# First layer of a four-stage model: loop over head pairs written out batch by batch, with the norms, gates and weight turning set between its steps

## The chip, the cores and the metric

The program runs on one core of a Trainium2 chip. Its engines work side by side and wait for each other by semaphores: TensorE (PE in the rows; PEld is its loading of weights), VectorE (DVE), ScalarE (ACT), GpSimd (POOL), and SyncE (SP), which here only issues transfers. PE's results go to PSUM, of which the kernel uses eight banks of 128 x 512 floats (`ps`); all other tiles named here are in SBUF. The metric is the device time of one execution in microseconds. Lower is better.

## The reference

The input `x` has 2 batches of 1024 tokens with 128 values, all in float32. Four stages follow each other, each as `x = x + layernorm(stage(layernorm(x)))`.

```python
def _L0_attn_ref(x, Wq, Wk, Wv):          # H, R = 8, 64; d = 128
    Q = (x @ Wq.T).reshape(b, n, H, R)
    K = (x @ Wk.T).reshape(b, n, H, R)
    V = (x @ Wv.T).reshape(b, n, H, d)
    attn = softmax(einsum('bnhr,bmhr->bhnm', Q, K), axis=-1)
    return einsum('bhnm,bmhd->bnd', attn, V)     # heads are summed

def _L0_ffn_ref(x, gate_w, w1, b1, w2, b2, w3, b3, sw1, sw2, sw3):   # E = 8 experts, top 2
    scores = softmax(xt @ gate_w.T)
    weights, idx = top_k(scores, 2)
    xs = xt[:, None, :] * weights[:, :, None]
    for e in range(E):
        y += sum((silu(xs @ w1[e].T + b1[e]) @ w2[e].T + b2[e]) * (xs @ w3[e].T + b3[e]) * (idx == e))
    z = silu(xt @ sw1.T) * (xt @ sw2.T) @ sw3.T
    return y + z
```

The third stage is a causal attention with 16 heads and a bias by distance. The fourth is two layers of windowed attention with a gated feed-forward. The change leaves these two as they are.

## The kernel before, in words

All of it is one function, `build`, with one instruction stream per engine, written by hand. The order in the code is the order on the engine, and nothing reorders it. What is late on one engine delays all that stands behind it there.

**First attention.** Two heads are a pair, and one pair of one batch is a block: 8 blocks. A loop over the 4 pairs (`Fori(0, PAIRS)`) holds two blocks, batch 0 and batch 1, so that q, k, v of one block are projected while the other still runs. GpSimd copies the pair's weights to fixed places (`a_weights`, `wq_st`, `wk_st`, `wv_st`). A block has 8 slots. In slot i PE makes the scores of 128 queries for both heads (`scores(i)`, L671, banks 0 to 3), turns two rows of probabilities made before (`turn`, L682, banks 4 and 5), and weights values with turned ones (`weigh`, L640). DVE takes the row maxima (L1269), ScalarE the exponentials with their sums (L1726), DVE divides (L1276), and both copy the turned halves back (`copy_out`). Each of PE's float32 products runs as two passes, and the rows count passes.

A block's output is 1024 queries in four quarters, c = 0 to 3, with two heads each: `weigh(m, b, c, head, k0, k1)` adds key tiles k0 to k1. Quarters 0 and 1 lie in the two halves of bank 6, quarters 2 and 3 in those of bank 7, and `add_out` (L1256) adds a full bank to `yT` on DVE. Quarter 2's second head and quarter 3 come only in the tail and in slots 0 to 2 of the next block. In block 0 the same code runs with nothing to weight: it works on cleared buffers. In the tail PE projects the next block's q (L609), k (L615) and v (L627); the last block projects a ninth one, which nobody uses.

```python
for i in range(QT):
    if i == 1:
        turn(0)
    scores(i)
    if i == 0:
        weigh(m - 1, 1 - b, 2, 1, 3, 8)
        weigh(m - 1, 1 - b, 3, 0, 0, 3)
    ...
    else:
        turn(2 * i - 2)
        weigh(m, b, (i - 3) // 2, (i - 3) % 2, 0, 6)
        turn(2 * i - 1)
        weigh(m, b, (i - 3) // 2, (i - 3) % 2, 6, 8)
```

**Ahead of it.** Both batches of `x` are loaded and normalised (`norm_in(0)`: DVE statistics L1171, ScalarE's root, DVE L1187, PE's transposes). PE turns the attention weights (L590) and all 31 blocks of expert and gate weights (L604, L601), and DVE copies these back.

**Behind it** come, one after the other, for all 16 tiles: `norm_out(0)` and the residual sum on GpSimd, `norm_in(1)`, the gate product (L733) and the choice of two experts on DVE, meanwhile the shared expert (`shared_up`, `shared_down`, L744 to L753), and the gate weights turned (L853). Then the experts: 32 units of one expert and 512 tokens, 16 for batch 0 and 16 for batch 1. In each PE spreads the gate's weights (L765, L766) and makes three products (L782, L788, L772), DVE has `scale`, a product with the mask, and `product`, ScalarE a copy and a Silu, and GpSimd sums into `yT` (`gather`, L2042). Norms of batch 0 behind the experts are already set between the units of batch 1 (`half_stats`, `half_aggr`, `half_norm`, `half_xn`), with the root as a power of -0.5 on GpSimd (`half_rstd`, L2050).

Of the kernel before, what the change touches and what calls it, by code (L numbers as in the profile page):

```python
# [13 lines left out]
P = 128  # L14
# [5 lines left out]
CH = 512  # L20
# [108 lines left out]
def build(nc, a, out):  # L129
    with ExitStack() as ctx:  # L130
# [16 lines left out]
        eps_c = sb("eps_c", [P, 1])  # L147
        ps = ctx.enter_context(nc.psum_tensor("ps", [P, 8, CH], F32))
# [12 lines left out]
        wq_st = sb("wq_st", [P, P])  # L161
        wk_st = sb("wk_st", [P, P])
        wv_st = sb("wv_st", [P, 256])

        w0qk = sb("w0qk", [P, 2, PAIRS + 1, P])
        w0q, w0k = w0qk[:, 0, :, :], w0qk[:, 1, :, :]
        w0v = sb("w0v", [P, PAIRS + 1, 256])
# [36 lines left out]
        gw = probs[:, 0, :].rearrange("p (n t e) -> p n t e", t=TILES, e=E0)  # L204
# [89 lines left out]
        s_ld_x = sem("s_ld_x")  # L294
# [18 lines left out]
        s_y = [sem(f"s_y{n}") for n in range(4)]  # L313
# [3 lines left out]
        s_a_wst = sem("s_a_wst")  # L317
# [17 lines left out]
        s_a_pz = sem("s_a_pz")  # L335
        s_a_oadd = sem("s_a_oadd")
        s_a_ozero = sem("s_a_ozero")
# [117 lines left out]
        def _(sp):  # L455
            for b in range(BATCH):
                sp.dma_start(x_sb[:, b * QT:(b + 1) * QT, :],
                             a["L0_attn_x"][b].rearrange("(t p) d -> p t d", p=P)).then_inc(s_ld_x, 16)
# [3 lines left out]
            sp.dma_start(wnat[:, 8:16, :], a["L0_attn_Wv"].rearrange("(n p) d -> p n d", p=P)).then_inc(s_ld_w0, 16)  # L462
# [67 lines left out]
            sp.wait_ge(s_y[2], 1)  # L530
# [23 lines left out]
        NU = 16  # L554
# [14 lines left out]
        def _(pe):  # L569
# [17 lines left out]
            pe.wait_ge(s_ld_w0, 16 * 4)  # L587
            for g in range(4):
# [3 lines left out]
            norm_in(0)  # L592

            pe.wait_ge(s_ld_f, 16 * 12)
            for g in range(9):
                if g < 4:
                    pe.wait_ge(s_w0t, 1)
                else:
                    pe.wait_ge(s_ft, g - 3)
                if g == 8:  # L600
                    ins = pe.transpose(ps[:, 4, 0:STRIP], gnat[:, :], ident[0:STRIP, 0:STRIP])  # L601
                else:
                    for i in range(min(4, 30 - 4 * g)):
# [9 lines left out]
            def a_proj_k(b):  # L613
# [1667 lines left out]
```

## Time and profile before

| | |
|---|---|
| median of 3 runs (lowest, highest) | 1608.4 us (1608.1, 1611.72) |
| the profiled execution, own time | 1610.09 us |
| its span, first to last instruction | 1608.0 us |
| instructions | 25414 |
| PE busy | 1383.7 us, 86% |
| DVE busy | 1049.2 us, 65% |
| ACT busy | 779.7 us, 48% |
| POOL busy | 387.2 us, 24% |
| mean granted clock of PE | 0.929 |
| PE's share of the chain that ended last | 62% |

Shares are means over stages with different limits, so the table says little on its own. The first attention, the gap behind it and the experts are read apart below. A granted clock of 1.00 is 2.4 GHz, of 0.50 is 1.2 GHz; a value between is a mean over a stretch that had both.

### The profile page before, as it was taken

To read this page: it belongs to the slowest core of one execution; us is meant where nothing else is said; L and a number is where in the kernel's file an instruction comes from. 1 tells how busy PE (TensorE), PEld (TensorE's weight loads), DVE (VectorE), ACT (ScalarE), POOL (GpSimd) and SP (SyncE) were. 2 spreads that over 40 slices of the span, in tenths; PEclk is the share of its full clock that TensorE was granted. 3 is DMA by queue.
4 is the path that set the end of the run, shared out by engine and by line. 5 is a ranking of instruction groups with operands and counts; after the bars stand their busy time and mean duration, and the time that the engine had idled before them with its cause. 6 is when DMAs were issued, how large, how long until landed. Compare 5 with 4: busy or idle time off the path is not lost.

```text
span 1608.0 us, 25414 instructions
## 1 busy us (share of the span) xinstructions
PE 1383.7 (86%) x9075; PEld 818.4 (51%) x9075; DVE 1049.2 (65%) x2238; ACT 779.7 (48%) x1658; POOL 387.2 (24%) x268
## 2 busy tenths in 40 slices
PE   6999999999999958997799999983688868788866
PEld 4777777777676733332233333322356643466542
DVE  6767767767676663666666676706688744788644
ACT  2444445444454413342245666663477743488731
POOL 2000000000000011345400000001588810688801
PEclk9999999999999978998678999997799979799978
DMA  5000000000000000002023111002000000000000
GB/s 132 1 1 1 0 0 0 0 0 0 0 0 0 0 0 0 1 1 92 12 74 86 40 46 44 5 2 60 1 1 0 1 1 1 1 0 0 1 0 26
DMA packets 23650, 25.44 MB, mean 16 GB/s; under 512 B 5570, under 2 KB 20108, under 8 KB 22284
## 3 DMA queue, kind: packets, MB, share of 16 engines
q1 hardware_dynamic: 23580, 24.51, 5.2%
q8 instruction: 44, 0.72, 0.2%
q14 instruction: 26, 0.21, 0.0%
HBM read 20.11 MB, written 4.39 MB: 15 GB/s over the span
## 4 chain that ended last, share of the span: by engine, by line
PE 62%; POOL 15%; DVE 10%; issue 7%; ACT 4%; DMA 2%; POOLq 0%; SPq 0%; DVEq 0%; ACTq 0%
PE ps L640 14%; PE ps L671 8%; PE ps L682 8%; POOL d_rn L2152 5%; PE ps L952 4%; POOL probsT L2163 4%; PE ps L911 4%; PE ps L932 3%; PE ps L788 2%; POOL q_st L2150 2%; POOL k_st L2150 2%; PE ps L782 2%; PE ps L627 2%; PE ps L772 2%; PE ps L1153 1%
## 5 line engine op out<-in xcount | busy, mean ns | idle before, releaser
L1881 ACT ACTIVATE probsT<-ps 128x512 f32<-128x512 f32 (+1 forms) x304 | 163.7, 576 | 111.0 <-PE ps L936 98.4
L1269 DVE TENSOR_REDUCE negmax<-ps 128x1 f32<-128x1024 f32 x128 | 150.8, 1220 | 76.1 <-PE ps L671 76.1
L1726 ACT ACTIVATE probs<-ps,negmax 128x1024 f32<-128x1024 f32 x128 | 142.8, 1115 | 75.8 <-DVE negmax L1269 75.5
L1732 ACT COPY probsT<-ps 128x512 f32<-128x512 f32 x128 | 75.0, 586 | 177.7 <-PE ps L682 177.7
L682 PEld LDWEIGHTS ps<-ident,probs 128*128 128x128 f32 x1024 | 114.7, 141 | 58.4 <-issue 53.5
L911 PE MATMUL ps<-arena 76*128 76x512 bf16 (+3 forms) x384 | 116.1, 363 | 26.8 <-DVE cmax L1477 20.4
L682 PE MATMUL ps<-ident,probs 128*128 128x128 f32 x1024 | 136.3, 276 | 0.0
L640 PE MATMUL ps<-probsT,v_nat 128*128 128x256 f32 x554 | 129.9, 380 | 0.0
L671 PE MATMUL ps<-k_st,q_st 64*128 64x512 f32 x512 | 127.2, 615 | 2.2 <-DVE v_st L1248 1.4
L1477 DVE CUSTOM_DVE_ANT_0 k_st<-ps,rel 128x256 f32<-128x256 f32 (+7 forms) x128 | 96.8, 756 | 47.9 <-PE ps L911 46.4
L1477 DVE CUSTOM_DVE_ANT_0 q_st<-ps,rel 128x256 f32<-128x256 f32 (+7 forms) x128 | 96.7, 756 | 45.2 <-PE ps L911 44.2
L932 PE MATMUL ps<-arena 79*128 79x512 bf16 (+3 forms) x384 | 115.1, 343 | 7.7 <-ACT probsT L1881 5.4
L640 PE MATMUL ps<-probsT,v_st 128*128 128x256 f32 x512 | 120.8, 380 | 0.0
L1954 ACT ACTIVATE probsT<-ps,d_nm,d_rn 128x128 f32<-128x128 f32 x256 | 113.4, 466 | 11.5 <-DVE d_nm L1611 11.5
L1282 DVE COPY probsT<-ps 128x512 f32<-128x512 f32 x128 | 87.9, 687 | 45.6 <-PE ps L682 44.6
L1996 POOL COPY wq_st<-w0qk 128x128 f32 (+1 forms) x5 | 1.5, 293 | 476.2 <-PE ps L671 463.6
L640 PEld LDWEIGHTS ps<-probsT,v_nat 128*128 128x128 f32 x554 | 100.9, 190 | 14.4 <-issue 3.0
L640 PEld LDWEIGHTS ps<-probsT,v_st 128*128 128x128 f32 x512 | 92.9, 190 | 13.3 <-issue 3.0
L1276 DVE TENSOR_SCALAR probs<-probs,rrow 128x1024 f32<-128x1024 f32 x128 | 96.4, 753 | 4.5
L1031 PE MATMUL ps<-arena 128*128 128x512 f32 x128 | 71.7, 689 | 30.0 <-ACT arena L1969 15.5
L2152 POOL TENSOR_TENSOR d_rn<-ss,half_c 128x16 f32<-128x16 f32 x32 | 93.1, 2910 | 0.4
L911 PEld LDWEIGHTS ps<-arena 76*128 76x128 bf16 x384 | 31.9, 102 | 101.7 <-DVE cmax L1477 71.2
(259 smaller groups left out, 2665.7 us busy)
## 6 DMA issues: line engine op xcount, KB each, us to landing
arena<-c_parts SPq DMA_DIRECT2D x32, 192.0 KB
arena<-c_parts SPq DMA_DIRECT2D x16, 128.0 KB
arena<-in_L_ffn_w_dram SPq DMA_DIRECT2D x3, 512.0 KB
c_parts<-probsT SPq DMA_DIRECT2D x2, 768.0 KB, 3.5
arena<-in_c_far_dram SPq DMA_DIRECT2D x16, 96.0 KB
c_parts<-work SPq DMA_DIRECT2D x2, 768.0 KB, 11.2
work<-in_L_ffn_wqkv_dram SPq DMA_DIRECT2D x1, 1536.0 KB
x_sb<-in_L_attn_x_dram SPq DMA_DIRECT2D x2, 512.0 KB, 4.8
```

Of the source, the lines that this page charges most:

```text
L640: ins = pe.matmul(ps[:, 6 + c // 2, (c % 2) * HC:(c % 2 + 1) * HC], a_v[b][:, kt, head * P:(head + 1) * P], a_pT[:, c % 2, head, kt, :], s ...
L671: ins = pe.matmul(ps[:, 2 * head + n, :], q_st[r:r + R0, i * P:(i + 1) * P], k_st[r:r + R0, n * CH:(n + 1) * CH], start=True, stop=True)
L682: ins = pe.transpose(ps[:, 4 + half, i * P:(i + 1) * P], probs[:, u % NPB, kt * P:(kt + 1) * P], ident[:, :])
L911: ins = pe.matmul(ps[:, 2 * (u % 2) + i, 0:e - i * CH], c_q2[buf][0:SHALLOW, j, qt * P:(qt + 1) * P], c_k2[buf][0:SHALLOW, j, i * CH:e], s ...
L932: ins = pe.matmul(ps[:, 4 + c % 2, i * n:(i + 1) * n], c_k2[buf][0:DEEP, j0 + i, kt * P:(kt + 1) * P], c_q2[buf][0:DEEP, j0 + i, q0:q0 + n ...
L1269: dve.tensor_reduce(negmax[:, u:u + 1], s2, AX_X, ALU.max, negate=True)\
L1276: dve.tensor_scalar(probs[:, u % NPB, :], probs[:, u % NPB, :], rrow[:, u:u + 1], None, ALU.mult).then_inc(s_a_norm, 1)
L1477: dve.tensor_tensor_reduce(c_dump[u % 2][:, 0:w], s2, rel[:, SEQ - w:SEQ], 1.0, -3.0e38, ALU.add, ALU.max, cmax[:, s % 2, m:m + 1]).then_i ...
L1726: act.activation(probs[:, u % NPB, :], s2, ACT.Exp, bias=negmax[:, u:u + 1], accum_out=rowsum[:, u:u + 1]).then_inc(s_a_exp, 1)
L1881: act.activation(c_p[:, kt % 2, j0:j0 + heads, q0 - kt * P:q0 - kt * P + n], ps[:, 4 + c % 2, 0:heads * n].rearrange("p (h n) -> p h n", n ...
L1954: ins = act.activation(d_p[:, par, h, :], ps[:, 6 + h // 4, (h % 4) * P:(h % 4 + 1) * P], ACT.Exp, bias=d_nm8[:, par, h:h + 1], scale=d_rn ...
L2152: pool.tensor_tensor(d_rn[:, par, :], ss[:, par, :], half_c[:, :], ALU.pow).then_inc(s_d_rn, 1)
```

## The change

The loop becomes plain code, `for m in range(BLOCKS)`, that runs all four pairs of batch 0 and then those of batch 1. Projections read the turned weights where they lie, and GpSimd's copies go. Block 0 skips the weighting of nothing, and the last block projects nothing.

At eight slots times eight blocks there are 64 numbered slots, and each of three engines has a function `a_piece(m, i)` that does at some of them a piece of other work: the nine groups of expert weights (PE in slots 0 to 6, 11 and 12, copied back by ScalarE in place of DVE), the input norm of batch 1 (14 to 22), the output norm of batch 0's attention (35 to 38), its next input norm (40 to 46), and its gates (51 to 63). Batch 1's output norm lies within the shared expert's products, and its next input norm and gates between the first 16 expert units. All pieces use bank 7. For that the quarters lie differently: 0, 1 and 2 one after another in the first half of bank 6, and only quarter 3 in bank 7, each read out by DVE on its own (256 columns), so that PE may start a quarter in bank 6 only when DVE has read the one before.

Batch 0 of `x` is asked for first and batch 1 behind the attention weights. ScalarE loads its tables by dummy operations at the start, and copies the turned wq and wk.

```diff
-            with pe.Fori(0, PAIRS) as p:
-                for b in range(BATCH):
...
+            for m in range(BLOCKS):
+                for i in range(QT):
+                    if i == 1:
+                        turn(m, 0)
+                    scores(m, i)
+                    if i == 0:
+                        weigh(m - 1, 2, 1, 6, 8)
+                        weigh(m - 1, 3, 0, 0, 6)
...
+                    a_piece(m, i)
+                if m + 1 < BLOCKS:
...
+                    a_proj_v(m + 1)
+                    weigh(m, 2, 1, 0, 6)
...
+                if k0 == 0:
...
+                    if c < 3 and head == 0 and 4 * m + c >= 1:
+                        pe.wait_ge(s_a_oadd, 4 * m + c if c else 4 * m - 1)
...
-                    ins = pe.matmul(ps[:, 6 + c // 2, (c % 2) * HC:(c % 2 + 1) * HC],
-                                    a_v[b][:, kt, head * P:(head + 1) * P],
+                    ins = pe.matmul(ps[:, 6 + c // 3, 0:HC],
+                                    a_v[m % 2][:, kt, head * P:(head + 1) * P],
...
+            def a_piece(m, i):
+
+                slot = QT * m + i
+                if slot < 7:
+                    turn_f(slot)
...
+                if slot == 51:
+                    gate(0, 0)
+                    gate(0, 4)
+                if slot == 62:
+                    turn_g(0, 0, 7)
...
-            a_weights(0)
```

**At the end of a block** PE's rows before are these, block 0 into block 1 (L627 projects v, L640 weights, L671 are scores, L682 turned probabilities, REGISTER_ALU the loop's counters):

```order
L627 MATMUL ps<-wv_st,xT 128x256 x8
L635 REGISTER_ALU
L640 MATMUL ps<-probsT,v_st 128x256 x3
L671 MATMUL ps<-k_st,q_st 128x512 x4
L640 MATMUL ps<-probsT,v_st 128x256 x5
L635 REGISTER_ALU
L640 MATMUL ps<-probsT,v_st 128x256 x3
L679 REGISTER_ALU
L682 MATMUL ps<-ident,probs 128x128 x8
```

and with the change (L669 projects v, L698 weights, L718 scores, L733 turned probabilities):

```order
L669 MATMUL ps<-w0v,xT 128x256 x8
L698 MATMUL ps<-probsT,v_st 128x256 x6
L718 MATMUL ps<-k_st,q_st 128x512 x4
L698 MATMUL ps<-probsT,v_st 128x256 x8
L733 MATMUL ps<-ident,probs 128x128 x8
L718 MATMUL ps<-k_st,q_st 128x512 x4
L733 MATMUL ps<-ident,probs 128x128 x8
L698 MATMUL ps<-probsT,v_st 128x256 x5
```

The tail weights six key tiles in place of three. Slot 0 keeps eight. Slot 1 weights five in place of seven (its rows before, x5 and x2, follow the ones shown), and slot 2 five in place of six.

**At the end of attention** PE's rows before run from the last projection of v to the first shared product (L583 and L575 turn the two norms, L733 is the gate product, L744 the shared expert):

```order
L627 MATMUL ps<-wv_st,xT 128x256 x8
L635 REGISTER_ALU
L640 MATMUL ps<-probsT,v_nat 128x256 x3
L654 REGISTER_ALU
L654 COMPARE_AND_BRANCH
L640 MATMUL ps<-probsT,v_nat 128x256 x21
L583 MATMUL ps<-ident,yT 128x128 x16
L575 MATMUL ps<-ident,xn 128x128 x16
L733 MATMUL ps<-gateT,xT 128x8 x16
L744 MATMUL ps<-xT,arena 128x512
```

and with the change (L733 and L698 as above, L756 turns gate weights, L861, L862 and L870 are the shared expert):

```order
L698 MATMUL ps<-probsT,v_nat 128x256 x2
L756 MATMUL ps<-ident,work 32x128 x4
L733 MATMUL ps<-ident,probs 128x128 x8
L698 MATMUL ps<-probsT,v_nat 128x256 x8
L733 MATMUL ps<-ident,probs 128x128 x8
L698 MATMUL ps<-probsT,v_nat 128x256 x16
L861 MATMUL ps<-xT,arena 128x512
L862 MATMUL ps<-xT,arena 128x512
L861 MATMUL ps<-xT,arena 128x512
L862 MATMUL ps<-xT,arena 128x512
L870 MATMUL ps<-probsT,arena 128x512
L619 MATMUL ps<-ident,yT 128x128 x8
```

The projection is gone, the two norms and the gate product stand earlier or later, and the shared expert follows the last weighting.

**DVE in a late slot of the last block**: before, any slot ended so (L1274 and L1276 divide, L1282 copies a turned half, L1269 are row maxima):

```order
L1274 RECIPROCAL rrow<-rowsum 128x1
L1276 TENSOR_SCALAR probs<-probs,rrow 128x1024
L1280 ISA
L1282 COPY probsT<-ps 128x4x128
L1274 RECIPROCAL rrow<-rowsum 128x1
L1276 TENSOR_SCALAR probs<-probs,rrow 128x1024
L1267 REGISTER_ALU
L1269 TENSOR_REDUCE negmax<-ps 128x1
```

and with the change slot 62 ends so (L1406 and L1408 divide, L1414 copies, L1396 adds a quarter, L1454 and L1455 write the last part of the gate weights, L1401 row maxima):

```order
L1406 RECIPROCAL rrow<-rowsum 128x1
L1408 TENSOR_SCALAR probs<-probs,rrow 128x1024
L1414 COPY probsT<-ps 128x4x128
L1406 RECIPROCAL rrow<-rowsum 128x1
L1408 TENSOR_SCALAR probs<-probs,rrow 128x1024
L1396 TENSOR_TENSOR yT<-ps,yT 128x256
L1454 CAST work<-work 128x64
L1455 CAST work<-work 128x8x8
L1401 TENSOR_REDUCE negmax<-ps 128x1 x2
```

Behind the second division stand a quarter's sum and two casts, for which PE's L756 of slot 62 waits.

## Rows read from the trace of the kernel before

**Rows 1.** Busy us (instructions) by stretch: PE, PEld, DVE, ACT, POOL; clock, DMA share, GB/s.

```profile
0.00:35.00 35.00, 19.41 (x87) 14.67 (x88) 22.27 (x73) 7.43 (x10) 9.10 (x14) 0.95 0.61 152
100.47:493.14 392.67, 391.99 (x2064) 282.54 (x2065) 277.61 (x408) 179.24 (x300) 2.61 (x9) 1.00 0.00 0
567.40:620.40 53.00, 28.84 (x109) 16.72 (x108) 30.77 (x171) 11.77 (x20) 7.00 (x6) 0.71 0.00 0
620.40:688.40 68.00, 67.57 (x160) 24.47 (x161) 40.27 (x69) 21.79 (x37) 22.22 (x18) 0.95 0.00 1
```

**Rows 2.** Timeline of PE, scores in block 0: start us, duration us, instruction.

```profile
35.03 1.99 PE L671 MATMUL ps<-k_st,q_st 64*128 64x512 f32 x8 [1.41 <-DVE v_st L1248]
41.62 1.99 PE L671 MATMUL ps<-k_st,q_st 64*128 64x512 f32 x8
47.59 1.99 PE L671 MATMUL ps<-k_st,q_st 64*128 64x512 f32 x8
54.00 1.99 PE L671 MATMUL ps<-k_st,q_st 64*128 64x512 f32 x8
...
83.09 1.99 PE L671 MATMUL ps<-k_st,q_st 64*128 64x512 f32 x8
100.47 1.09 PE L671 MATMUL ps<-k_st,q_st 64*128 64x512 f32 x3
```

**Rows 3.** Timeline, all engines, slot 6 of block 0.

```profile
77.73 1.09 PE L682 MATMUL ps<-ident,probs 128*128 128x128 f32 x8
77.83 2.36 DVE L1269 TENSOR_REDUCE negmax<-ps 128x1 f32<-128x1024 f32 x2 [1.23 <-PE ps L671]
78.66 2.76 PE L640 MATMUL ps<-probsT,v_st 128*128 128x256 f32 x12
...
80.30 1.11 ACT L1726 ACTIVATE probs<-ps,negmax 128x1024 f32<-128x1024 f32 x1
...
83.12 0.75 DVE L1276 TENSOR_SCALAR probs<-probs,rrow 128x1024 f32<-128x1024 f32 x1
```

**Rows 4.** Timeline, tail of block 0.

```profile
90.27 1.88 PE L609 MATMUL ps<-xT,wq_st 128*128 128x512 f32 x4
...
95.45 3.62 PE L627 MATMUL ps<-wv_st,xT 128*128 128x256 f32 x16
...
99.11 1.22 DVE L1248 COPY v_nat<-ps 128x1024 f32<-128x1024 f32 x1 [1.91 <-PE ps L627]
```

**Rows 5.** Timeline of DVE, first norm, and the second norm's scaling.

```profile
6.73 3.19 DVE L1171 BATCH_NORM_STATS2 stats<-x_sb 128x6 f32<-128x128 f32 x16 [5.84 <-DMA x_sb<-in_L_attn_x_dram]
9.96 1.17 DVE L1174 BATCH_NORM_AGGREGATE mv<-stats 128x2 f32<-128x6 f32 x16
...
584.36 4.20 DVE L1187 TENSOR_SCALAR xn<-x_sb,mv,rstd 128x128 f32<-128x128 f32 x16
```

**Rows 6.** Timeline, end of attention to the shared expert.

```profile
557.01 10.52 PE L640 MATMUL ps<-probsT,v_nat 128*128 128x256 f32 x48
...
590.40 4.45 PE L733 MATMUL ps<-gateT,xT 128*128 128x8 f32 x32 [0.67 <-ACT xT L1693]
...
603.78 1.28 ACT L1761 ACT_TABLE_LOAD   x1 [7.93 <-DVEq L1345]
```

**Rows 7.** Timelines, expert units 18 to 20 with a norm between them.

```profile
694.95 1.02 PE L782 MATMUL ps<-probsT,arena 128*128 128x512 f32 x2
...
697.83 1.66 POOL L2050 TENSOR_TENSOR rstd<-rstd,half_c 128x8 f32<-128x8 f32 x1
698.26 1.02 PE L782 MATMUL ps<-probsT,arena 128*128 128x512 f32 x2
...
699.46 1.26 POOL L2042 TENSOR_TENSOR yT<-yT,probsT 128x512 f32<-128x512 f32 x1
699.52 3.07 DVE L1443 TENSOR_SCALAR xn<-x_sb,mv,rstd 128x128 f32<-128x128 f32 x8 [0.21 <-POOL rstd L2050]
...
703.25 1.13 PE L782 MATMUL ps<-probsT,arena 128*128 128x512 f32 x2
```

More of the change, by code:

```diff
@@ new lines, in gate @@
+            def gate(b, t0):
+                if t0 == 0:
+                    pe.wait_ge(s_xT, group_no(1, b, 1))
+                    if b == 0:
+                        pe.wait_ge(s_a_oadd, 24)
+                for t in range(t0, t0 + 4):
+                    ins = pe.matmul(ps[:, 7, t * E0:(t + 1) * E0], xT[:, (QT * b + t) * P:(QT * b + t + 1) * P],
+                                    gateT[:, :], start=True, stop=True)
+                if t0 == 4:
+                    ins.then_inc(s_logits, 1)
@@ L1203, in norm_out, with half_stats, half_aggr, out_stats @@
                         ins.then_inc(s_yn, 1)
+            def half_stats(kind, k, b, g, src):
+                for i in range(4):
+                    ch.link(dve.bn_stats(stats[:, QT * b + 4 * g + i, :], src(i)))
+            def half_aggr(b, g=None):
+                part = tiles_of(b, g)
+                ch.settle()
+                for t in range(part.start, part.stop):
+                    ins = dve.bn_aggr(mv[:, t, :], stats[:, t, :])
+                ins.then_inc(s_hvar, 1)
+            def out_stats(k, b, g, bank):
+                dve.wait_ge(s_yp, group_no(k, b, g))
+                half_stats("out", k, b, g, lambda i: ps[:, bank, i * P:(i + 1) * P])
@@ new lines, in gate_scores, with gate_best @@
+            def gate_scores(b):
+                half = tiles_of(b)
+                dve.wait_ge(s_gexp, b + 1)
+                ch.step(dve.tensor_reduce(gsum[:, half], gw[:, 1], AX_X, ALU.add))
+                ch.step(dve.reciprocal(gmax[:, half], gsum[:, half]))
+                ch.step(dve.tensor_tensor(gw[:, 2], gw[:, 1], per_token(gmax[:, half]), ALU.mult))
+            def gate_best(b):
+                for t in range(QT):
+                    ch.link(dve.max(gw[:, 3, t, :], gw[:, 2, t, :]))
+                ch.settle()
@@ L1345, in _ @@
-            dve.sem_inc(s_G, 1)
+            in_stats(0, 0, 0)
+            in_stats(0, 0, 1)
+            ch.settle()
+            for t in range(QT):
+                ins = dve.bn_aggr(mv[:, t, :], stats[:, t, :])
+            ins.then_inc(s_var, 1)
+            dve.wait_ge(s_sd, 1)
+            ch.step(dve.reciprocal(rstd[:, 0:QT], sd[:, 0:QT]))
+            half_xn(0, 0, 0, 0)
+            half_xn(0, 0, 1, 0)
+            turned_w0(0)
+            turned_w0(1)
+            a_evac_k(0)
+            a_evac_v(0)
@@ L1347, in shared @@
+            add_out(BLOCKS - 1, 2)
+            add_out(BLOCKS - 1, 3)
             def shared(k):
@@ L1426, in _ @@
+            units(0, UB, piece)
             shared(4)
```

1002 lines of the change are left out of this document (576 added, 426 removed).

## The prediction

> **What bounds the kernel now.** I read the stages first, in the table of busy time by stretch [rows 1]. Blocks 1 to 6 of the first attention keep TensorE (PE) at work 391.99 of 392.67 us at a granted clock of 1.00, its level of 2.4 GHz. Whoever shortens that part must take PE work out. On either side lie 35.0 us before the first scores, and 53.0 us between the last weighting (567.4) and the first expert unit (620.4), in which PE is busy for 28.8 us at a clock of 0.71. Those two gaps need only better order.
>
> Second, the starts of the scores in block 0: eight slots and a tail [rows 2]. Slots 0, 1 and 2 take 6.59, 5.97 and 6.41 us; the four from 54.00 to 83.09 take 7.27 each; slot 7 with the tail takes 17.38. The next block begins 65.44 us after this one, and the six blocks of [rows 1] take 392.67, again 65.44 each. A pass of the loop holds two blocks, so a branch back costs nothing that can be seen, and writing the loop out gains nothing by itself.
>
> Third, one steady slot [rows 3], S (75.81) being the start of its scores, 7.28 ahead of the next ones. PE's work in it: scores 4 x 0.43 (two heads side by side), 16 transposes of 0.107, 16 passes of 0.215, together 6.9 of the 7.27. VectorE (DVE) sat idle for 1.23 us before the row maxima, which end at S+4.38. ScalarE's second exponential then needs 1.1, and its sum lands near S+5.7, where PE wants it at S+7.27. So per slot DVE has 1.23 us idle, and may be some 1.3 us late beyond that before PE waits. The chain's 5.7 us is also the shortest slot.
>
> **The start.** DVE begins its statistics at 6.73, when both halves of x are in; 16 tiles take 3.19 [rows 5]. With one batch asked for first I take x at 4.9 (it then shares the queues with less), and go by halves of the rows: statistics 1.6, aggregation 0.6, root and reciprocal 0.7, eight normalisations 2.1, so 9.9. The last four transposes and their copy end at 11.5, and the eight transposes of Wv, which the code puts ahead of the projections, at 12.6. Then come the projections, 1.9 + 1.9 + 3.6 [rows 4], hence first scores at 20.5 in place of 35.03: **-14.5**. The 30 turned expert weights and DVE's clearings leave this path. Bounds: all projections at half clock, 7 later (-7.5); x sooner, -16.
>
> **Attention.**
> - The eighth block no longer projects a ninth: 1.72 + 1.72 + 3.44 = **-6.9** [rows 4].
> - Block 0 weighted nothing useful 21 times (42 passes, 9 us of PE). But slot 0 waits for its first normalised row anyway, and slots 1 and 2 cannot go under 5.7. That leaves 0.25 + 0.7, **-0.9**.
> - Six passes move into the tail, four leave slot 1, two leave slot 2 (the order above). The tail was all but covered: the second half of v is copied by 100.33, scores start at 100.47 [rows 4, 2]. So the tail grows by 6 x 0.215 less 0.15 = 1.1. Slot 1 gives back 0.25 (then the chain holds it), slot 2 0.43. Net 0.45 at each of 7 boundaries, **+3.2**.
> - Pieces on PE. Nine groups of turned weights, of which the six in slots 3 to 6, 11 and 12 count, 2.4 in all; those in slots 0 to 2 lie in PE's new gaps. Eight groups of four transposes for norms and gates at 0.45, 3.6. The gate product of one batch, half of 4.45, so 2.2 [rows 6]. Sum 8.2; nothing can cover them in slots where PE is the bound.
> - Pieces on DVE. Four statistics take 0.8 and four normalisations 1.05 [rows 5]; from PSUM I estimate 1.3, for a gate step 0.5 to 0.7, and for a quarter of the output 0.4 in every second slot. All of DVE's work in the seam was 30.8 for both batches [rows 1], so one batch's norms and gates are at most 15, spread over 30 slots. They lie in the 1.23 of idle time and the 1.3 of play. Slots 16, 40 and 41 are themselves short, and I give them 1.3. Slot 62 is the exception: PE turns the gate weights at the end of its slot, but DVE writes the last part of them only behind its own last multiply, which ends at S'+0.8 (S' = start of the next scores [rows 3]), a quarter and two casts. That is 1.7 of wait on PE. With PE's 8.2: **+11.2**.
> - Slots 0 to 2 of block 0 now leave PE idle half of the time. Where it idled in the seam, its clock was 0.71 [rows 1]. I charge **+3.0** for one or two spells at 1.2 GHz (0 to 8).
>
> **The seam.** Of the 53.0 us, batch 1's output norm and four shared products stay behind the last weighting. Counted from it: first product 0.9, table load 1.28 [rows 6], Silu 0.6, DVE's product 0.7; PE goes on with batch 1's transposes, three more pairs of products and down products. The third of these waits for ScalarE's copy of y, at +11. DVE: statistics until +7.5, aggregation until +8.1; POOL's root, 1.66 [rows 7] and a short sum ahead of it, until +10.3; eight normalisations until +12.9, the last product, the first scaling at +14.3. First unit at +14.6, so 14.6 - 53.0 = **-38.4**. If the root is not waited for, it is -40; if all of it runs at half clock, -32.
>
> **First 16 expert units.** A unit takes 3.31 where nothing is put in [rows 7]. The second half of the experts already carries such a norm: the unit with eight normalisations and eight transposes took 4.99, which prices the same piece in the first half at +1.7. The gate product adds 2.2 and turning the gate weights 0.9. Around the one Exp stand two table loads of 1.28; ScalarE has room for half of them before Silu is late, +1.3. Other steps 0.4: **+6.5**.
>
> In that unit eight normalisations took 3.07 where they take 2.10 alone (half of 4.20), and a sum on POOL of 1.26 us ran at their start [rows 7, 5]. The Trainium skill (SBUF — State Buffer, Who interferes with whom) states that DVE in a two-port mode and GpSimd hold one pair of ports in turn, each for a whole instruction; by that rule, the row agrees. By it the four residual sums that POOL now makes during attention could each hold up DVE's multiply for a whole sum, and the total would be up to 5 us worse if nothing covered it. By the slot's rows its play covers one such hold-up, and I leave the sum as it is.
>
> **The sum.** -14.5 - 6.9 - 0.9 + 3.2 + 11.2 + 3.0 - 38.4 + 6.5 = -36.8. Behind the 16th unit nothing moves but wait counts and banks' names. The profiled execution took 1610.1 us (span 1608.0), so it becomes 1573.3; it lay 1.7 above the median, so I forecast a median of **1572**. Less than 0.3% (5 us) from 1608.4 cannot be told from no change.
>
> **Rivals.**
> 1. *As summed*, 1565 to 1581: 0.62.
> 2. *DVE's play is too small, or PE's clock falls.* Slots 35 to 38 carry 1.3 us each against 0.85 or 1.23 of idle time, and POOL's hold-ups come on top; or PE, thinner in places, is granted half clock for longer. For it: DVE is busy 277.6 of 392.7 us as it is [rows 1]. Against: each overrun is small and an empty slot wins back 1.2. Price: 0.25 us in each of 64 slots (16), or three spells of 10 us at half the speed (15): 1582 to 1592, 0.18.
> 3. *More is hidden.* The pieces on PE fill the 0.4 of gaps per slot, the clock stays up, x lands early. Then 11.2, 3.0 and 6.5 shrink by half: 1553 to 1564, 0.14.
> 4. *Slower: quarters share a bank.* Quarters 0, 1 and 2 of every block now build up in one half bank, and PE may not start one before DVE has read the last. By the slot, DVE is through at S'+1.2 and PE starts at S'+2.85: 1.6 us of margin at 24 hand-overs. This decides only where each read comes 3.4 us later than I reckon (1.75 beyond the margin, 24 x 1.75 = 42 us against 37 gained): 1614 or more, 0.04. For it stands that DVE works in strict order, so that a late piece delays the read as well.
> 5. *Nothing moves*: the seam's work comes back inside attention at full price. Against it, 24 of the 53 us were PE's idle time: 1608, 0.02.
>
> Chances: faster 0.94, same 0.02, slower 0.04. The range, 1559 to 1587, takes in the start at half clock (+7) and half of case 2, and the pieces at nothing (-13).
>
> **What would show it.** Right: first scores at 20 to 21 us; later blocks of 65.9 plus their pieces, with empty slots 3 to 6 still at 7.27 and tails longer by 1.1; PE waiting for DVE some 1.7 us in slot 62; the last weighting's end near 560, the first expert unit near 575, the 17th near 648, and all behind as before but 40 us earlier. Wrong: slots of 7.5 or more with DVE as releaser, PE waits on the reads of quarters, half clock inside attention, or a seam over 20 us.

## The result, and the profile after

The changed kernel takes 1568.12 us in the median of 4 runs (1564.41 to 1569.39), the kernel before 1608.25 in as many on the same chip: a ratio of 0.9744, 95% interval 0.9721 to 0.9768. Forecast were 1572 and a range of 1559 to 1587. Measured once more beside later kernels it took 1568.45 (0.9736, 0.9714 to 0.9758).

Its profiled execution took 1564.41 us, span 1562.6. Busy time by stretch, with the columns of [rows 1]:

```profile
0.00:19.40 19.40, 12.04 (x48) 8.73 (x48) 7.23 (x30) 7.64 (x11) 0.30 (x5) 1.00 0.99 244
19.40:88.65 69.25, 62.69 (x338) 44.48 (x337) 46.86 (x69) 33.67 (x57) 0.99 (x3) 0.98 0.04 9
88.65:491.82 403.17, 397.96 (x2110) 287.60 (x2109) 292.30 (x500) 181.78 (x308) 9.48 (x12) 1.00 0.00 1
561.60:576.30 14.70, 12.67 (x35) 5.31 (x34) 8.45 (x30) 4.74 (x7) 5.31 (x5) 0.96 0.00 0
576.30:650.60 74.30, 70.41 (x194) 26.91 (x192) 53.99 (x134) 27.19 (x45) 25.16 (x22) 0.99 0.00 1
```

Start and seam are short, and the stretches between are longer. To see where, take the start of each slot's scores (L718 on PE) and of each expert unit (L901) and subtract. The starts of the eight blocks and the 17th unit, in both kernels, worked out so from the timelines:

```
            first  block 1  2       3       4       5       6       7       weighting ends  unit 1  unit 17
before      35.03  100.47   165.92  231.37  296.81  362.25  427.69  493.14  567.54          620.44  688.49
after       19.41  88.65    155.44  222.90  289.19  356.34  423.86  491.82  561.61          576.31  650.60
```

The start, in the timelines of DVE and PE ([rows 5, 4] are the counterparts):

```profile
5.23 1.64 DVE L1329 BATCH_NORM_STATS2 stats<-x_sb 128x6 f32<-128x128 f32 x8 [4.33 <-DMA x_sb<-in_L_attn_x_dram]
...
8.15 2.14 DVE L1364 TENSOR_SCALAR xn<-x_sb,mv,rstd 128x128 f32<-128x128 f32 x8
...
12.42 1.88 PE L648 MATMUL ps<-xT,w0qk 128*128 128x512 f32 x4
...
19.41 1.99 PE L718 MATMUL ps<-k_st,q_st 64*128 64x512 f32 x8
```

Before, PE's timeline had the turned expert weights ahead of the projections, which began at 25.41, and a wait within them:

```profile
20.46 4.79 PE L604 MATMUL ps<-ident,arena 128*128 128x128 f32 x30 [2.42 <-DVE w0v L1218]
...
31.62 1.99 PE L627 MATMUL ps<-wv_st,xT 128*128 128x256 f32 x8 [0.79 <-DVE k_st L1244]
```

So 13.0 of the 15.6 us lie ahead of the projections and 2.6 behind their start.

In attention an empty slot 3 to 6 takes 7.27 as before. The boundary of two blocks and the first slots of the next, in the timeline of PE (blocks 0 and 1; [rows 2, 4] are their counterparts):

```profile
77.33 1.88 PE L648 MATMUL ps<-xT,w0qk 128*128 128x512 f32 x4
...
82.51 3.62 PE L669 MATMUL ps<-w0v,xT 128*128 128x256 f32 x16
85.96 2.75 PE L698 MATMUL ps<-probsT,v_st 128*128 128x256 f32 x12
88.65 1.99 PE L718 MATMUL ps<-k_st,q_st 64*128 64x512 f32 x8
...
95.19 1.99 PE L718 MATMUL ps<-k_st,q_st 64*128 64x512 f32 x8
...
100.86 1.99 PE L718 MATMUL ps<-k_st,q_st 64*128 64x512 f32 x8 [0.50 <-ACT probs L1944]
102.78 1.09 PE L733 MATMUL ps<-ident,probs 128*128 128x128 f32 x8
103.70 1.46 PE L698 MATMUL ps<-probsT,v_st 128*128 128x256 f32 x6
105.00 0.60 PE L733 MATMUL ps<-ident,probs 128*128 128x128 f32 x4
105.89 0.66 PE L733 MATMUL ps<-ident,probs 128*128 128x128 f32 x4 [0.28 <-DVE probsT L1414]
106.38 1.03 PE L698 MATMUL ps<-probsT,v_st 128*128 128x256 f32 x4
107.34 1.99 PE L718 MATMUL ps<-k_st,q_st 64*128 64x512 f32 x8
```

Twelve passes now stand in the tail, where six stood. Slot 1 (from 95.19) takes 5.67, slot 2 (from 100.86) 6.48: it has two passes fewer than before, yet is no shorter than the old 6.41. The old slot 2 (from 113.03), in PE's timeline before:

```profile
115.87 2.32 PE L640 MATMUL ps<-probsT,v_st 128*128 128x256 f32 x10
118.03 1.04 PE L682 MATMUL ps<-ident,probs 128*128 128x128 f32 x8
118.91 0.60 PE L640 MATMUL ps<-probsT,v_st 128*128 128x256 f32 x2
```

The second half of the slot's last turning needs VectorE's copy, and that copy stands behind both row maxima. Before, ten passes stood ahead of this turning and PE came to it late enough not to wait; two stood behind. Now six stand ahead, PE waits 0.28 there (105.89), and four stand behind. So of the 0.86 us of the four passes taken out ahead, about half is lost at the wait, and the two passes added behind it cost 0.43: nothing is left.

Slot 62, the last weighting and the seam, same view, with [rows 6] as counterpart; the turning of the gate weights is L756, the unit's first product L901:

```profile
538.65 1.03 PE L698 MATMUL ps<-probsT,v_nat 128*128 128x256 f32 x4
541.17 0.61 PE L756 MATMUL ps<-ident,work 128*32 128x128 f32 x4 [1.50 <-DVEq L1459]
541.71 1.99 PE L718 MATMUL ps<-k_st,q_st 64*128 64x512 f32 x8
...
554.53 7.07 PE L698 MATMUL ps<-probsT,v_nat 128*128 128x256 f32 x32
561.44 1.02 PE L861 MATMUL ps<-xT,arena 128*128 128x512 f32 x2
...
571.46 1.10 PE L870 MATMUL ps<-probsT,arena 128*128 128x512 f32 x2 [0.40 <-ACT yT L2004]
...
574.73 1.80 PE L870 MATMUL ps<-probsT,arena 128*128 128x512 f32 x2 [1.63 <-DVE probsT L1552]
576.31 1.91 PE L901 MATMUL ps<-probsT,arena 128*128 128x512 f32 x2
```

### The profile page after: what moved, and what is told of

Its sections match the earlier page's. It is cut to its first block, busy times and chain, and to the rows that moved or that the text cites. A ratio compares the mean times of both kernels' runs of the same rounds, so it can differ in the third digit from the quotient of the medians.

```text
span 1562.6 us, 24586 instructions
## 1 busy us (share of the span) xinstructions
PE 1352.1 (87%) x9009; PEld 799.1 (51%) x9009; DVE 1042.3 (67%) x2249; ACT 782.3 (50%) x1668; POOL 386.9 (25%) x264
## 4 chain that ended last, share of the span: by engine, by line
PE 58%; POOL 16%; DVE 11%; issue 8%; ACT 5%; DMA 1%; POOLq 0%; SPq 0%; DVEq 0%; ACTq 0%
PE ps L698 12%; PE ps L718 8%; PE ps L733 6%; POOL d_rn L2383 5%; PE ps L1070 4%; POOL probsT L2394 4%; PE ps L1029 4%; PE ps L1050 3%; POOL q_st L2381 2%; DVE negmax L1401 2%; POOL k_st L2381 2%; PE ps L907 2%; PE ps L901 2%; PE ps L669 2%; PE ps L1273 2%
## 5 line engine op out<-in xcount | busy, mean ns | idle before, releaser
L1401 DVE TENSOR_REDUCE negmax<-ps 128x1 f32<-128x1024 f32 x128 | 150.7, 1219 | 72.3 <-PE ps L718 72.1
L733 PEld LDWEIGHTS ps<-ident,probs 128*128 128x128 f32 x1024 | 114.7, 141 | 66.0 <-issue 43.8
L733 PE MATMUL ps<-ident,probs 128*128 128x128 f32 x1024 | 138.6, 277 | 6.6 <-DVE probsT L1414 3.3
L718 PE MATMUL ps<-k_st,q_st 64*128 64x512 f32 x512 | 128.5, 620 | 5.9 <-ACT probs L1944 5.9
L698 PE MATMUL ps<-probsT,v_st 128*128 128x256 f32 x512 | 120.8, 380 | 0.0
L698 PE MATMUL ps<-probsT,v_nat 128*128 128x256 f32 x512 | 120.2, 380 | 0.0
L2195 ACT ACTIVATE probsT<-ps,d_nm,d_rn 128x128 f32<-128x128 f32 x256 | 113.4, 467 | 11.6 <-DVE d_nm L1803 11.6
L1414 DVE COPY probsT<-ps 128x512 f32<-128x512 f32 x128 | 87.7, 685 | 43.4 <-PE ps L733 43.3
L698 PEld LDWEIGHTS ps<-probsT,v_st 128*128 128x128 f32 x512 | 92.9, 190 | 13.3 <-issue 3.0
L698 PEld LDWEIGHTS ps<-probsT,v_nat 128*128 128x128 f32 x512 | 93.1, 190 | 12.7 <-issue 2.3
L1408 DVE TENSOR_SCALAR probs<-probs,rrow 128x1024 f32<-128x1024 f32 x128 | 96.4, 753 | 4.5
## 6 DMA issues: line engine op xcount, KB each, us to landing
c_parts<-work SPq DMA_DIRECT2D x2, 768.0 KB, 11.2
```

Source lines behind the costliest of these rows:

```text
L698: ins = pe.matmul(ps[:, 6 + c // 3, 0:HC], a_v[m % 2][:, kt, head * P:(head + 1) * P], a_pT[:, c % 2, head, kt, :], start=(head == 0 and k ...
L718: ins = pe.matmul(ps[:, 2 * head + n, :], q_st[r:r + R0, i * P:(i + 1) * P], k_st[r:r + R0, n * CH:(n + 1) * CH], start=True, stop=True)
L733: ins = pe.transpose(ps[:, 4 + half, i * P:(i + 1) * P], probs[:, u % NPB, kt * P:(kt + 1) * P], ident[:, :])
L1401: dve.tensor_reduce(negmax[:, u:u + 1], s2, AX_X, ALU.max, negate=True).then_inc(s_a_negmax, 1)
L1408: dve.tensor_scalar(probs[:, u % NPB, :], probs[:, u % NPB, :], rrow[:, u:u + 1], None, ALU.mult).then_inc(s_a_norm, 1)
L2195: ins = act.activation(d_p[:, par, h, :], ps[:, 6 + h // 4, (h % 4) * P:(h % 4 + 1) * P], ACT.Exp, bias=d_nm8[:, par, h:h + 1], scale=d_rn ...
```

## The experiments

All started from one of the two kernels. The times are medians (of one run each in 6 and 8); the ratios are to the kernel before on the same chip, 0.9744 (0.9721 to 0.9768) for the changed kernel, and as the chips differ they compare kernels better than the times. The slots and units are worked out from the timelines of the profiled executions, as above.

**1. The loops written out, nothing else** (kernel before).

```diff
-            with pe.Fori(0, PAIRS) as p:
+            for p in range(PAIRS):
```
(and the same for the other three engines)

> The kernel before, with the four loops over pairs of blocks written out and nothing else changed: same instructions in the same order, waits on constants in place of registers. Theory (the prediction's reading that the branch back costs nothing): every block still takes 65.44 us and the time stays at 1608.3, within 2 us. Rival A (the branch did cost something on some engine's path): blocks 1 to 6 fall under 65.3 and the time by 1 us or more. Rival B (straight code has to be fetched all the time and that costs): blocks grow past 65.6, the time by 1 us or more, with idle time of PE that no semaphore ends.

Measured: 1607.99 against 1609.98, ratio 0.9993 (0.9971 to 1.0014). Blocks 1 to 6 take 65.37 in place of 65.44; the 0.08 comes off slot 0 of blocks 1 to 7, also where no branch lies ahead, so it is not the branch. The blocks stay between the bounds of Rivals A and B; the whole time cannot tell them apart.

**2. Without useless passes and ninth projection** (kernel before, written out). The passes left out had also cleared part of the bank that the first addition reads, so part of the output is off in this kernel.

```diff
+                if m < 0:
+                    if c == 3 and k1 == QT and head == 1:
+                        pe.sem_inc(s_a_pv, 1)
+                    return
...
-                    a_proj_q(nb)
+                    if not last:
+                        a_proj_q(nb)
```

> The kernel before, written out, and without the 42 passes of block 0 that weight nothing useful and without the ninth projection and its four evacuations. Theory (terms of the prediction): 6.9 less at the end of block 7 and 0.9 less in block 0, so 7.8 us faster, 1600.5, last weighting's end at 559.7 in place of 567.5. Rival A: only the ninth projection counts (-6.9, block 0 unchanged), because slots 0 to 2 of block 0 wait for the first normalised rows or fall to half clock when PE idles there. Rival B: the ninth projection covered ScalarE's and VectorE's last steps, so that only part of 6.9 comes back (-4 or less).

Measured: 1600.87, ratio 0.9947 (0.9927 to 0.9967), 7.1 below the one before. From the start of block 7 to the last weighting's end it is 68.00 in place of 74.32, -6.3. But slots 0 to 2 of block 0 take 6.91, 6.99 and 5.67, 0.6 more than the 18.97 before: a spell at half clock, 3.4 us long from 41.5, fell on the scores of slot 1. Rival A holds for block 0. Part of what block 7 lacks to 6.9 is a wait of 0.33 for ScalarE's copy at its last turning (PE, 550.11), now that no projection lies ahead of it. In the profiled execution the seam also grew by 3.2 (27.3 us at half clock on end behind 567.2, where it was 17.1 and 6.8); the medians do not show that.

**3. Both halves of x first** (changed kernel).

```diff
             load_x(0)
+            load_x(1)
             sp.dma_start(ident[:, :], a["c_ident"]).then_inc(s_ld_w0, 16)
```
(and the later `load_x(1)` taken out)

> The changed kernel, with both batches of x asked for first, as before the change, and the weights of q, k and v behind them. It tells how much of the earlier start comes from asking for one batch alone. Theory: VectorE's statistics begin at 5.23 in the changed kernel and began at 6.73 before; with both halves ahead they begin between 5.3 and 6.7 and the weights land later too, so first scores move from 19.4 to 20.5 to 21.5: 1 to 2 us slower. Rival A: the first half lands as soon as before, since the order in the queue alone decides it, and only the weights come later; the first scores are held by the weights or not at all, 0 to 0.5 us. The rest of the 15.6 us (the turned expert weights and the clearings off the path, half as many tiles) stays in both.

Measured: 1568.59, ratio 0.9753 (0.9734 to 0.9772), no difference to the changed kernel that the runs could tell. In the profiled execution the first scores start at 20.39 in place of 19.41. VectorE's statistics begin at 5.22, as in the changed kernel (5.23). The weights come later, as the timeline of PE shows, first of the changed kernel, then of this one:

```profile
7.23 1.97 PE L625 MATMUL ps<-ident,probsT 128*128 128x128 f32 x8 [7.23 <-DMA probsT<-in_L_attn_Wk_dram]
```
```profile
9.07 1.97 PE L625 MATMUL ps<-ident,probsT 128*128 128x128 f32 x8 [9.07 <-DMA probsT<-in_L_attn_Wk_dram]
```

So asking for one batch gives some 1.0 of the 15.6 us, and by way of the weights. The 1.0 is one pair of profiles: in the nine profiles with the changed order (the changed kernel, its repeat and the runs from 4 on) the first scores start between 18.96 and 19.85, and this turning between 6.88 and 7.40. The order of the queue, not the amount in it, sets when the first half of x is there: the mechanism is Rival A's, with the theory's size. That VectorE could begin 1.5 earlier than before has another cause: before, it waited for both halves.

**4. The old split of passes at the boundary** (changed kernel).

```diff
-                        weigh(m - 1, 2, 1, 6, 8)
-                        weigh(m - 1, 3, 0, 0, 6)
+                        weigh(m - 1, 2, 1, 3, 8)
+                        weigh(m - 1, 3, 0, 0, 3)
...
-                    weigh(m, 2, 1, 0, 6)
+                    weigh(m, 2, 1, 0, 3)
```
(slots 1 and 2 likewise)

> The changed kernel, with the passes of quarters 2 and 3 at a block's boundary divided as before the change (3 in the tail, 5+3 in slot 0, 5+2 in slot 1, 5 and 1 in slot 2). Theory (from the slots as they now stand in the profile): tail 17.4 in place of 18.5, slot 1 back from 5.67 to 5.96, slot 2 back from 6.48 to 6.41, so 0.84 less at each of 7 boundaries, 5.9 us faster. Rival A (the prediction's own term): 0.45 at each, 3.2 us faster. Rival B: with quarters 0 to 2 in one half bank the old split makes PE wait for VectorE's read of quarter 2, and nothing is won or up to 3 us lost.

Measured: 1560.15, ratio 0.9698 (0.968 to 0.9716), 8.0 below the changed kernel (7.4 by the ratios). Tails 17.39, slot 1 at 5.96, slot 2 at 6.41, and no new wait. The last weighting ends 6.8 earlier. Against the kernel before, this part of the change was a loss of 0.84 at each of seven boundaries, 5.9. Against this run it is 0.91, 6.4 in all, because the 0.84 also holds what slot 0 gains in straight code (run 1). The other 0.5 comes from slots 1 and 2 of blocks 2 and 5, which lie behind pieces (6.80 to 6.41 in block 5).

**5. Batch 0's gates behind attention** (changed kernel): product, shift, exponential, choice, parts and turning leave slots 51 to 63; VectorE does them ahead of `shared(2)`.

> The changed kernel, with batch 0's gates (product, shift, exponential, best two, index, the three parts, turning) taken out of slots 51 to 63 and put behind the last weighting, between the shared products; the norms stay inside attention. It asks what hiding the gates was worth. In attention they cost PE 1.69 in slot 51, 2.11 in slot 62 and 0.44 in slot 63, so 4.2 us come back there. In the seam VectorE's gate work is 6.7 us (sum of its rows in slots 52 to 62), of which 2 us fit into its wait for GpSimd's root; then PE's turning and two copies by ScalarE follow, 1.3. Theory: the seam grows from 14.7 to 21 us (20 to 23), net 2 us slower than the changed kernel. Rival A (the seam has room beside VectorE, so that the gates cost little there): seam under 18, net faster by 1 or more. Rival B (the chain of gate steps is one of waits, not of work): seam of 26 or more, net slower by 7 or more, with half clock in it as before.

Measured: 1574.73, ratio 0.9777 (0.9748 to 0.9807), 6.6 slower than the changed kernel (5.3 by the ratios, whose intervals overlap; in the profiled executions the 17th unit starts 8.2 later). The last weighting ends at 557.42, 4.2 earlier, as expected. The seam takes 26.3, not 21: Rival B, though the net loss of the medians stays just under its 7. The timeline shows that ScalarE has its Exp, which needs the gate product, ahead of the table load and the Silus, and that each later step waits for the one before:

```profile
560.69 1.85 PE L740 MATMUL ps<-gateT,xT 128*128 128x8 f32 x16
...
563.36 1.28 ACT L1984 ACT_TABLE_LOAD   x1
...
566.19 2.04 PE L858 MATMUL ps<-probsT,arena 128*128 128x512 f32 x2 [3.66 <-DVE probsT L1532]
568.03 1.91 PE L619 MATMUL ps<-ident,yT 128*128 128x128 f32 x8
...
578.32 1.53 PE L858 MATMUL ps<-probsT,arena 128*128 128x512 f32 x2 [2.96 <-DVE probsT L1532]
```

The table load begins 5.9 us behind the last weighting (before this edit 0.1). PE waits 3.7 us for the first down product, half clock comes with it (6.8 us of it, from 565.2), and the norm's turning (L619) begins 10.6 us behind the last weighting where it began at 4.1, so that its root and all behind come late. 6.7 us of VectorE's work and 1.9 + 0.9 of PE's (product and turning) make the seam 11.6 longer; how much of the 11.6 is the half clock and how much the chain, this run does not separate.

**6. GpSimd's first three sums left out** (changed kernel).

```diff
+                if k in (0, 1, 2):
+                    pool.sem_inc(s_e_y, 1)
+                    return
                 pool.tensor_tensor(y, y, e_t[:, k % 2, :], ALU.add).then_inc(s_e_y, 1)
```

> The changed kernel, leaving out GpSimd's sums of the first three expert units' results (1.27 us each; the output lacks these units), waits and counts kept. It asks why unit 3 takes 5.96 us where 5.0 was forecast: there VectorE's eight normalisations take 4.03 us, while two of GpSimd's sums run. Theory (the two engines hold each other up in the memory they share): the eight take 2.1 to 2.2, and unit 3 falls to 4.1 to 4.9. Rival (VectorE's late start or its own order makes the unit long): the normalisations stay at 3 to 4 us or the unit stays at 5.7 or more.

Measured: unit 3 (units counted from 0) takes 4.18 for 5.96. First the eight normalisations of the changed kernel with the sums on GpSimd (timelines of both engines; in [rows 7] one sum met eight such, and they took 3.07), then those of this kernel:

```profile
588.14 1.27 POOL L2289 TENSOR_TENSOR yT<-yT,probsT 128x512 f32<-128x512 f32 x1
589.58 1.29 POOL L2289 TENSOR_TENSOR yT<-yT,probsT 128x512 f32<-128x512 f32 x1 [0.17 <-POOL yT L2289]
588.21 4.03 DVE L1364 TENSOR_SCALAR xn<-x_sb,mv,rstd 128x128 f32<-128x128 f32 x8 [0.23 <-POOL rstd L2256]
```
```profile
589.56 2.14 DVE L1364 TENSOR_SCALAR xn<-x_sb,mv,rstd 128x128 f32<-128x128 f32 x8 [0.22 <-POOL rstd L2256]
```

Two of eight last 1.3 us each, a whole sum, where one takes 0.33. The theory is shown: 1.9 us of VectorE's time, and 1.8 of the unit's. The time of this kernel, 1568.59 in its one run, says nothing: units 0 and 1 were 1.6 longer in it (6.8 us at half clock from 575.9).

**7. Quarters read 3.6 us later** (changed kernel).

```diff
                     rowmax(m, u + 1)
+                    if i % 2 == 1:
+                        add_out((4 * m + i // 2 - 2) // 4, (i // 2 - 2) % 4)
```
(and the call at the end of the even slots taken out)

> The changed kernel, with VectorE's read of each quarter of the output moved from the end of an even slot to behind the row maxima of the next one. It puts the prediction's slow rival (quarters share a bank) into effect. In the changed kernel the read ends 1.72 before PE starts the next quarter; moved, it ends 3.6 later, 1.9 beyond the margin. Two hand-overs per block have so little room, quarter 0 to 1 in slot 5 and 1 to 2 in slot 7; from 2 to the next block's 0 there are two slots. Theory: PE waits some 1.9 in slots 5 and 7 of each block, 16 times, of which an empty slot gives nothing back: 25 to 32 us slower than the changed kernel. Rival A (24 hand-overs, as the prediction counted): 40 us or more. Rival B (the work behind catches up, since VectorE and ScalarE have slack in a slot): PE waits, but slots grow by under 1 us, less than 15 us in all.

Measured: 1603.26 (1601.41 to 1611.18), ratio 0.9964 (0.9946 to 0.9983), 35 slower than the changed kernel; in the profiled execution the 17th unit starts 40.1 later. PE's timeline in slot 5 of block 1, and of block 2:

```profile
130.75 2.83 PE L698 MATMUL ps<-probsT,v_nat 128*128 128x256 f32 x12 [1.84 <-DVE yT L1396]
```
```profile
201.75 4.51 PE L698 MATMUL ps<-probsT,v_st 128*128 128x256 f32 x12 [1.84 <-DVE yT L1396]
```

Slot 5 and slot 7 with its tail each grow by 2.08, in all blocks: 16 hand-overs, 33 us. The theory had the mechanism and the count, and its 25 to 32 us were too few: a slot grows by more than its wait, and the work behind catches up nothing. Four of those slots grow by some 1.7 more. In each of these four lies a spell of 3.4 us at half clock (from 201.9, 345.2, 509.1 and 563.7), and twelve passes take 4.51 where they take 2.76.

**8. PE filled in slots 0 to 2 of block 0** (changed kernel).

```diff
+                    if m == 0 and i < 3:
+                        for r in range(8):
+                            pe.matmul(ps[:, 6, 0:HC], a_v[0][:, 4 + r % 4, 0:P], xT[:, 0:HC],
+                                      start=True, stop=True, skip_group_check=True)
```

> The changed kernel, with eight more passes of 256 columns on PE at the end of slots 0, 1 and 2 of block 0, whose result is overwritten unread. It asks what the half clock at 25.5 us costs and whether PE's idle time brings it. Now the three slots take 6.92, 6.94 and 6.05. Theory: PE is idle nearly half of the time there; with the passes in its gaps (0.86 a slot) the spell at half clock goes away or moves, and the slots come down to 6.6, 5.9, 6.0, so 1 to 1.5 us less in all. Rival A: the spell stays, whatever PE does behind the scores, and the passes cost their own time at half clock: 1 to 3 us more. Rival B: spell gone, but the slots stay at about 6.9, because VectorE's and ScalarE's chain holds them.

Measured: 1571.54 in one run, slower and not faster. There is no half clock before 578.8, but the slots take 6.83, 6.83 and 9.51. Each of these products is two passes, so the filling cost 3.62 a slot and not the 0.86 that I wrote: more than the gap holds, and in slot 2 all of it is paid. With PE filled the spell is gone, so PE's idle time brings it; on its price the run says nothing.

**9. Three edits together** (changed kernel): the old split; part 1 of the gate weights in slot 60, part 2 in 61; four such products, 1.89 us, in slots 0 and 1 of block 0.

> The changed kernel with three small edits: the old split of passes at a block's boundary, part 1 of batch 0's gate weights moved from slot 61 to 60 and part 2 from 62 to 61, and four products (eight passes, 1.8 us) on PE at the end of slots 0 and 1 of block 0, overwritten unread. Theory: the split gives 6.8 (as its own run showed at the 17th unit), the parts take VectorE's last one out of PE's path in slot 62 (9.38 to 7.7, -1.67), the passes lie wholly in PE's 3 us of idle time and keep the clock at 1.00, so that slots 0 and 1 take 6.5 and 5.9 (-1.4). 17th unit at 640.7 in place of 650.6, time 1558. Rival A (slot 62): the turning waits for something else than the last part, and stays over 9 us. Rival B (the clock): four products are too few, the spell at half clock stays, and slots 0 and 1 sum to 13.8 as before or more.

Measured: 1556.87 (1556.05 to 1557.33), ratio 0.9663 (0.9642 to 0.9685), 17th unit at 640.07. All three came out. Slot 62 takes 7.71, and the turning follows the weighting without a wait:

```profile
529.82 1.03 PE L698 MATMUL ps<-probsT,v_nat 128*128 128x256 f32 x4
530.68 0.60 PE L756 MATMUL ps<-ident,work 128*32 128x128 f32 x4
531.22 1.99 PE L718 MATMUL ps<-k_st,q_st 64*128 64x512 f32 x8
```

The filling costs nothing, and slots 0 and 1 take 6.54 and 5.66 at a clock of 1.00:

```profile
21.59 1.89 PE L836 MATMUL ps<-xT,v_st 128*128 128x256 f32 x8
24.70 1.09 PE L733 MATMUL ps<-ident,probs 128*128 128x128 f32 x8 [1.22 <-DVE probs L1412]
25.73 1.99 PE L718 MATMUL ps<-k_st,q_st 64*128 64x512 f32 x8
```

In the changed kernel a wait of 2.95 stood there, and the scores behind it fell into the spell from 25.5:

```profile
24.93 1.47 PE L733 MATMUL ps<-ident,probs 128*128 128x128 f32 x8 [2.95 <-DVE probs L1408]
26.33 3.25 PE L718 MATMUL ps<-k_st,q_st 64*128 64x512 f32 x8
```

**10. Normalisations dealt out over two units** (on top of 9).

> The one before, and batch 1's eight normalisations of unit 2 dealt out over two units (four on VectorE behind unit 2, four behind unit 3, turned on PE in units 3 and 4), with the gate's product a unit later. Theory: GpSimd's two queued sums then hold up one normalisation each at most while VectorE has a unit's slack for each half; units 3 and 4 take 4.0 to 4.3 each in place of 5.96 and 3.41, so 1 us less (0.5 to 1.5), and the gate's shift by a unit moves nothing. Rival A: unit 3 stays at 5 or more, since both sums still fall into the first four: nothing gained. Rival B: the later gate steps now pile up in unit 7 or the last two and cost 1 us or more there.

Measured: 1558.13, ratio 0.9667 (0.9645 to 0.969): no gain. Units 3 and 4 take 4.93 and 3.89 in place of 5.95 and 3.40, so 0.5 less. Both sums still fall into the first four normalisations, as Rival A has it (its bound, 5 or more for unit 3, was just missed):

```profile
579.44 3.00 DVE L1367 TENSOR_SCALAR xn<-x_sb,mv,rstd 128x128 f32<-128x128 f32 x4 [0.22 <-POOL rstd L2259]
```

GpSimd begins its queued sums with the end of the same root for which VectorE waits, so the first share meets them however the rest is dealt out. One of the other four meets a third sum (2.05 for four, from 584.27). Units 0 and 1 were 2.0 longer in this execution (6.8 us at half clock from 565.9; in 9 it was 3.4).

**11. The changed kernel again.**

> The changed kernel once more, beside the two above on one chip. It asks how much of its time behind the 17th unit is chance. In its first profile that stretch took 912.0 us, in the profile of the kernel before 919.5, with a spell of 17.1 us at half clock at 869.7 that the changed kernel had not. Theory (the spell belongs to an execution, not to a kernel): 17th unit again at 650.6 within 0.5, stretch behind it between 912 and 919, median 1566 to 1570. Rival (the changed kernel avoids it by its work): stretch again 912.0 within 0.5.

Measured: 17th unit at 650.79, the stretch behind it 915.8. The theory holds: 912.0 belonged to one execution.

## Why the prediction was right, point by point

The median came out 4 us under the forecast, by the mechanism forecast; the profiled execution 8.9 under its 1573.3. Up to the 17th unit the sum was -36.8 and -37.9 was measured (688.49 to 650.60). That is closer than its terms: they miss by -1.1 (start), -1.2 (block 0 and clock), +2.7 (split), -1.4 (pieces), +0.2 (seam) and -0.3 (units), which cancel by chance. The signs "near 560", "near 575" and "near 648" don't follow from the sum, which puts the last weighting's end at 562.6, the first unit at 577.2 and the 17th at 651.7; measured were 561.6, 576.3 and 650.6.

- **The start**, -14.5: measured -15.6. VectorE began at 5.23 for the 4.9 supposed, and the projections at 12.42 for 12.6. The rest is in these: back to back they start 1.72, 1.72 and 3.55 apart, and I had added up the 1.9, 1.9 and 3.6 that the rows give them, whose ends overlap. Another 0.5 is a slip, for 12.6 + 1.9 + 1.9 + 3.6 is 20.0 and not 20.5. Run 3 took back only the order of the loads; that the expert weights and the clearings left the path is read from the timelines and was not tried alone. Run 3 corrects a reason: x does not come sooner for sharing its queues with less, VectorE merely waits for one half and not for two.
- **Block 7**, -6.9: it took 69.79 for 74.40, pieces 2.55 more and its first slots 0.27 less, hence -6.9. Run 2 alone gave -6.3.
- **Block 0's useless passes** (-0.9) **and the clock** (+3.0): together +2.1, measured +0.9 (19.91 for 18.97). Run 9 separates them: without a spell the three slots take 18.25, -0.7, so the one spell cost 1.7.
- **The split**, +3.2: the mis-sized term. It is +5.9 (6.4 against run 4, which took it back). The tail (+1.1) and slot 1 (-0.29) were right. The step that failed is "slot 2 gives back 0.43". I took passes out of a slot as if PE were its bound; PE there waits inside the slot for VectorE's copy, and of the passes behind that copy there were two more, not fewer. The slot grew by 0.07.
- **Pieces**, +11.2: 9.8. Turned groups in slots 3 to 6 cost 0.44 each as forecast, those in 11 and 12 only 0.22 and 0.18, and a small product in 13, not in the sum, 0.12; the gate product 1.69 for 2.2; the pieces of slots 16, 40 and 41, which show in the slots behind them, together 0.66 for 1.3. VectorE's norms were wholly covered: slots 35 to 38 of 64 grew by nothing but their transposes' 0.44. Slot 62's wait, 1.7, came as described (1.67, run 9).
- **The seam**, -38.4: 14.7 for 52.9, so -38.2. The waits come in the order forecast and some 0.5 earlier (root until +9.8 for +10.3, normalisations until +12.5 for +12.9), and the last down product then runs at half clock, 1.80 where it takes 1.02, which the sum did not have. Run 5 took back the gates alone: they were worth 11.6 of the seam, more than their duration. The norms and the shared products, the larger part, no run took back.
- **First 16 units**, +6.5: +6.2, but errors cancel. Unit 3 cost 2.65 for 1.7, since two sums and not one hit the normalisations; VectorE's last gate steps made units 11 and 12 longer by 1.4, where "other steps" had 0.4; the gate product took 1.7 for 2.2; units 0 and 1 were 1.8 shorter than before, since the shorter seam left only 3.4 us at half clock for 6.8.
- **Behind the 17th unit**, 0: 912.0 in this profile, 919.5 in that of before. Half clock for 17.1 us at 869.7 in the one has no counterpart in the other; run 1 lacks it too (916.2). By the medians of the runs some 2 us are left of this, no more than profiles of one kernel differ by, and what they hang on stays open.

**The rivals.** Case 2 did not come: no slot shows VectorE late except 62, and slots 17 and 42, which grew by 0.3 each. Its hold-ups by GpSimd during attention did not occur either. Only two residual sums fall into attention, not four, and both ran beside row maxima, as the timelines of both engines in block 4 show for the first:

```profile
325.33 1.27 POOL L2263 TENSOR_TENSOR x_sb<-x_sb,xn 128x512 f32<-128x512 f32 x1 [6.75 <-DVE xn L1355]
325.17 2.35 DVE L1401 TENSOR_REDUCE negmax<-ps 128x1 f32<-128x1024 f32 x2
```

Each maximum took 1.22 as ever. The Trainium skill (SBUF — State Buffer, Who interferes with whom) names both sides: scaling can take the shared ports, where a reduction never does on this chip. Runs and rows agree, 0.33 to 1.3 us for the one and no change for the other. Not every scaling is held up: in the seam eight that read PSUM took 0.41 each, with the other two residual sums beside them and without (VectorE 571.43 to 574.07, the sums from 572.88). Case 3 did not come: the turned groups of slots 3 to 6 cost their full 0.44. Case 4 was well priced in kind: the read's margin is 1.72 in the changed kernel (1.6 forecast), and run 7 shows that the 1.9 beyond it is paid in full. But its count was wrong, for only 16 of the 24 hand-overs are close; the third has two slots of room. By an estimate from these, 37 us over 16 on top of 1.72 makes 4.0 us of lateness to use up the gain, not 3.4.

## What to carry to other kernels

Work of the bound engine taken out ahead of a slot's last wait pays in part or not at all, and work added behind that wait is paid in full: look for what PE waits for inside the slot before moving work across a boundary. A chain of short dependent steps in a seam can cost more than its busy time (11.6 us for 9.5 here, half clock included); inside a loop that has slack, the same steps cost 4.2, of which 1.7 was a wait that run 9 took out. Deal such pieces out so that the last part is done a slot ahead of its use, and check what GpSimd does at that moment.

## What the chip showed that was not expected

- Half clock followed short waits of PE inside otherwise full work: 3.4 us of it beside a wait of 2.95 in the changed kernel, and behind four of the 16 waits of 1.84 in run 7. It cost 1.26 us on four scores (3.25 for 1.99) and 1.75 on twelve passes. Overwritten products of 1.89 us in such a gap removed it.
- Half clock far behind the edit differs between executions: the stretch behind the 17th unit took 912.0 and 915.8 in two of the changed kernel, and 912.0 to 919.5 over all profiles here, though its work is the same. Such a difference between two profiles says nothing on a change.
- A normalisation of 0.33 us on VectorE, from SBUF to SBUF, took 1.3 us when it began beside a GpSimd sum of 1.27 (run 6); one that reads PSUM took no longer.
